# Softmax denominators of a cross-attention: sums of probability tiles on VectorE and GpSimd in place of ones matmuls

## What is computed

```python
# per batch element and head; q: 512 x 8, k and v: 154 x 8 (218 x 8 in layer 0)
s = q @ k.T / sqrt(8)                      # masked keys get -inf
p = exp(s - max(s, axis=keys))             # unnormalised probabilities
o = (p @ v) / sum(p, axis=keys)            # the denominator is what the change touches
x = x + concat_heads(o) @ Wo + bo
```

## Time and profile before

| | |
|---|---|
| median of 3 runs | 964.61 us (962.47 to 964.93) |
| the profiled execution | 964.95 us |
| its span, first to last instruction | 963.2 us |
| attention items of layers 0 and 1 | 46 to 363 us |
| feed-forward of layer 1 | 363 to 540 us |
| attention items of layer 2 | 540 to 656 us |
| feed-forward of layer 2, then layer 3 | 656 to 963 us |
| instructions | 15428 |

### The profile page before, as it was taken

One profiled execution on the slowest core, in us unless ns is written; L12 is line 12 of the kernel. 1 busy time (PEld: TensorE's weight loads), 2 busy tenths in 40 slices (PEclk: granted clock), 3 DMA queues, 4 the chain that ended last, 5 costly groups with the idle time before them and its releaser, 6 DMA issues. The chain is left out here.

```text
span 963.2 us, 15428 instructions
## 1 busy us (share of the span) xinstructions
PE 890.3 (92%) x5522; PEld 635.3 (66%) x5522; DVE 574.8 (60%) x1401; ACT 444.9 (46%) x799; POOL 275.6 (29%) x402
## 2 busy tenths in 40 slices
PE   3799999999999998999989899998999999999994
PEld 3555464655565536889877655545888888888783
DVE  2866758574866756454546477765536344454478
ACT  7265574757574654243322456755224232222350
POOL 6321407263766441011111145432001000021152
PEclk9999999998999999999999899999999999999997
DMA  5000000001020110000000210100000000000001
GB/s 159 7 2 15 1 17 1 15 2 37 2 56 11 71 37 24 1 1 1 1 1 1 81 36 26 53 25 14 2 1 1 1 1 1 2 1 1 1 1 44
DMA packets 27573, 18.10 MB, mean 19 GB/s; under 512 B 6221, under 2 KB 25770, under 8 KB 27370
## 3 DMA queue, kind: packets, MB, share of 16 engines
q1 hardware_dynamic: 27498, 17.12, 6.3%
HBM read 15.63 MB, written 1.05 MB: 17 GB/s over the span
## 5 line engine op out<-in xcount | busy, mean ns | idle before, releaser
L1377 DVE TENSOR_REDUCE mneg<-PS 128x2 f32<-128x308 f32 (+1 forms) x384 | 180.1, 515 | 107.2 <-PE PS L913 106.3
L1848 ACT ACTIVATE work<-PS 128x512 f32<-128x512 f32 (+2 forms) x168 | 100.0, 597 | 249.0 <-PE PS L1104 235.3
L1546 DVE TENSOR_TENSOR work<-PS,work 128x512 f32<-128x512 f32 (+2 forms) x168 | 114.8, 685 | 166.3 <-PE PS L1104 122.6
L1825 ACT ACTIVATE work<-PS 124x512 f32<-124x512 f32 (+1 forms) x272 | 157.1, 601 | 89.3 <-PE PS L1039 88.2
L1118 PEld LDWEIGHTS PS<-down_w,work 128*128 128x128 f32 (+2 forms) x1344 | 157.9, 191 | 5.7 <-DVE work L1546 1.3
L1118 PE MATMUL PS<-down_w,work 128*128 128x128 f32 (+2 forms) x1344 | 158.5, 275 | 1.0 <-DVE work L1546 1.0
L1102 PE MATMUL PS<-xh_sb,arena 128*128 128x512 f32 (+2 forms) x336 | 138.0, 411 | 8.8 <-DVE work L1546 8.7
L1104 PE MATMUL PS<-xh_sb,arena 128*128 128x512 f32 (+2 forms) x336 | 132.7, 395 | 0.0
L1103 PE MATMUL PS<-xl_sb,arena 128*128 128x512 f32 (+2 forms) x336 | 132.1, 393 | 0.0
L1926 POOL TENSOR_SCALAR rstd<-bn_mv 128x4 f32<-128x4 f32 x32 | 7.6, 238 | 423.1 <-DVE bn_mv L1275 423.0
L913 PEld LDWEIGHTS PS<-kb_sb,qxt_sb 97*128 97x128 f32 x256 | 44.0, 190 | 61.6 <-DVE mneg L1377 28.7
(11 more groups left out here) (217 smaller groups left out, 1248.5 us busy)
## 6 DMA issues: line engine op xcount, KB each, us to landing
ctx_rep<-in_ctxT SPq DMA_DIRECT2D x12, 308.0 KB, 3.3
stage<-in_w SPq DMA_DIRECT2D x8, 256.0 KB, 3.9
stage<-in_wg SPq DMA_DIRECT2D x8, 176.0 KB, 2.5
stage<-in_wu SPq DMA_DIRECT2D x8, 176.0 KB, 2.4
x_res<-in_x SPq DMA_DIRECT2D x4, 256.0 KB, 5.4
down_w<-in_w SPq DMA_DIRECT2D x1, 1024.0 KB
down_w<-in_wd SPq DMA_DIRECT2D x8, 128.0 KB
out<-x_res SPq DMA_DIRECT2D x4, 256.0 KB, 2.3
```

Of the source, the lines that this page charges most:

```text
L1377: dve.tensor_reduce(mneg[:, a % 2, t, h0:h0 + 2], PS[:, bank_of["mx", a, m], 0:2 * (KT0 if layer == 0 else KC)].rearrange("p (h n) -> p h ...
L1546: dve.tensor_tensor(HH[0:rows, e % 2, j, :], PS[0:rows, 2 * (n % 2) + 1, :], SS[0:rows, n % 2, :], ALU.mult).then_inc(*sig["h"].mark((i, n)))
L1825: act.activation(p_tile(i, n)[0:rows, :], PS[0:rows, n % 2, :], ACT.Exp, scale=SCALE).then_inc(*sig["p"].mark((i, n)))
L1848: act.activation(SS[0:rows, n % 2, :], PS[0:rows, bank, :], ACT.Silu).then_inc(*sig["act"].mark((i, n)))
```

## The change

The keys are padded from 154 to 160 and laid out in chunks of 32 keys times four heads, so every chunk has 128 rows and row r belongs to head r // 32 in all of them: 5 chunks of context keys, and 2 more of memory keys in layer 0. The six padding keys get a bias that makes their probability zero. As all chunks have the same layout, the denominators can be formed from the sum of the tiles. For each head group, DVE or POOL adds the tiles of all chunks but the last (`p_sum`), slot by slot; PE applies the 0/1 matrix `MV` once to that sum (slot N - 1) and once to the last chunk's tiles (slot N + 3). The sum for slot m is queued one slot later; which engine does it is in `on_vector`: in layer 0 DVE does 11 and POOL 9, in layers 1 and 2 DVE and POOL do 6 each. An `exps` now waits for the value matmul and for the sum that read the tile before. The maxima are 320 or 448 columns wide. `v_blocks` in layer 0 needs 7 matmuls in place of 13. The replicated context comes from the host in its final layout (`ctxR`), there is one small DMA more (`pad`), and some memsets at the start are gone. Some entries of the slot tables move by one to five slots. The diff, cut to its core:

```diff
+KP = 160
+KH = KP // 2
+KPC = 32
+CC = KP // KPC
...
-R0, C0 = 125, 7
-R1, C1 = 124, 5
-KT0 = KC + KM
+RK = HL * KPC
+C0 = CC + KM // KPC
+C1 = CC
...
+        P3SUM = sb("p_sums", [128, 3, S])
...
+        P_SUM = [P3SUM[:, 0, :], P3SUM[:, 1, :], P3SUM[:, 2, :], work[:, 4096:4608]]
...
+        def on_vector(m):
+
+            return m in (4, 5, 7, 11, 13, 15, 19, 20, 21, 22, 23)
+
+        def sum_signal(m):
+
+            return sig["p_sum_dve" if on_vector(m) else "p_sum"]
+
+        def p_sum(eng, i, m):
+
+            g = m % G
+            eng.wait_ge(*sig["p"].at((i, m)))
+            if m < 2 * G:
+                u = after(i, -1)
+                if is_attn(u):
+                    eng.wait_ge(*sig["dn"].at((u, n_slots(u) - G - 1)))
+                    if g == G - 1:
+                        eng.wait_ge(*on_signal(u).at(u))
+                elif u is not None:
+                    eng.wait_ge(*sig["resid"].at(u))
+            else:
+                eng.wait_ge(*sum_signal(m - G).at((i, m - G)))
+            eng.tensor_tensor(P_SUM[g], p_tile(i, m - G) if m < 2 * G else P_SUM[g], p_tile(i, m), ALU.add).then_inc(
+                *sum_signal(m).mark((i, m)))
...
-                if n % 4 == 3 and n >= 7:
+                if n in (N - 1, N + 3):
                     c = (n - 7) // 4
...
+                        if not last:
+                            pe.wait_ge(*sum_signal(4 * c + g).at((i, 4 * c + g)))
+                        pe.matmul(PS[32 * g:32 * g + 32, 7, :], MV[:, :], p_tile(i, 4 * c + g) if last else P_SUM[g],
+                                  start=not last, stop=last).then_inc(*sig["dn"].mark((i, 4 * c + g)))
...
                 if n >= P_RING:
-                    act.wait_ge(*sig["dn"].at((i, n - P_RING)))
+                    act.wait_ge(*sig["pv"].at((i, n - P_RING)))
+                    m = max(n - P_RING, n % G + G)
+                    act.wait_ge(*sum_signal(m).at((i, m)))
...
+                act.wait_ge(*sig["dn"].at((i, n_slots(i) - G - 1)))
                 act.activation(VS, PS[:, 6, :], ACT.Copy).then_inc(*sig["vs"].mark(i))
...
+                    m = n - 1
+                    if kind == "A" and G <= m < n_slots(i) - G and on_vector(m):
+                        p_sum(dve, i, m)
...
+                    m = n - 1
+                    if ITEMS[i][0] == "A" and G <= m < n_slots(i) - G and not on_vector(m):
+                        p_sum(pool, i, m)
```

More of the change, by code:

```diff
@@ L144, in n_slots @@
     if kind == "A":
[L145 removed]
+        return 4 * chunks_of(layer)
     return {"F0": 4, "F1": 16, "F2": 26, "A3": 4, "F3": 2}[kind]
@@ L837, in v_blocks @@
                 layer, b = a // B, a % B
-                rows, chunks = chunk_shape(layer)
                 if part == 0:
@@ L845, in v_blocks @@
                 wait_for(bank)
-                for c in range(4 * part, min(4 * part + 4, chunks)):
-                    o = PS[0:rows, bank, (c % 4) * D:(c % 4 + 1) * D]
-                    cols = slice(c * rows, (c + 1) * rows)
-                    mem = layer == 0 and (c + 1) * rows > KC
-                    mm = pe.matmul(o, CR[:, a % 2, cols], WA[:, layer % 2, 2, :], start=True, stop=not mem)
-                    if mem:
-                        mm = pe.matmul(o, MR[:, cols], ident[:, :], start=False, stop=True)
+                for c in range(4 * part, min(4 * part + 4, chunks_of(layer))):
+                    o = PS[0:RK, bank, (c % 4) * D:(c % 4 + 1) * D]
+                    if c < CC:
+                        mm = pe.matmul(o, CR[:, a % 2, c * RK:(c + 1) * RK], WA[:, layer % 2, 2, :], start=True, stop=True)
+                    else:
+                        mm = pe.matmul(o, MR[:, c - CC, :, :].rearrange("p h n -> p (h n)"), ident[:, :], start=True, stop=True)
                 mm.then_inc(*sig["v_psum"].mark((a, part)))
@@ L1023, in attention_step @@
                 a = layer * B + b
-                rows, chunks = chunk_shape(layer)
+                chunks = chunks_of(layer)
                 N = 4 * chunks
@@ L1038, in attention_step @@
                         pe.wait_ge(*taken[n % 2])
-                    pe.matmul(PS[0:rows, n % 2, :], KB(layer)[0:K_ALL, a % 2, g, c * rows:(c + 1) * rows],
+                    pe.matmul(PS[0:RK, n % 2, :], KB(layer)[0:K_ALL, a % 2, g, c * RK:(c + 1) * RK],
                               QXT[0:K_ALL, a % 2, g, :], start=True, stop=True).then_inc(*sig["st"].mark((i, n)))
@@ L1050, in values @@
                 a = layer * B + b
-                rows, chunks = chunk_shape(layer)
+                chunks = chunks_of(layer)
+                N = 4 * chunks
                 if n % 4 == 1 and n >= 5:
@@ L1063, in values @@
                         taken[6] = sig["vs"].at(i) if is_attn(after(i, 1)) else on_signal(i).at(i)
-                if n % 4 == 3 and n >= 7:
+                if n in (N - 1, N + 3):
                     c = (n - 7) // 4
-                    mask = MV0 if layer == 0 else MV1
-                    if c == 0 and 7 in taken:
+                    last = n == N + 3
+                    if not last and 7 in taken:
                         pe.wait_ge(*taken[7])
                     for g in range(G):
-                        pe.matmul(PS[32 * g:32 * g + 32, 7, :], mask[0:rows, c, :], p_tile(i, 4 * c + g)[0:rows, :],
-                                  start=(c == 0), stop=(c == chunks - 1)).then_inc(*sig["dn"].mark((i, 4 * c + g)))
+                        if not last:
+                            pe.wait_ge(*sum_signal(4 * c + g).at((i, 4 * c + g)))
+                        pe.matmul(PS[32 * g:32 * g + 32, 7, :], MV[:, :], p_tile(i, 4 * c + g) if last else P_SUM[g],
+                                  start=not last, stop=last).then_inc(*sig["dn"].mark((i, 4 * c + g)))
                     if c == chunks - 1:
@@ L1297, in v_mask @@
                 layer = a // B
-                rows, chunks = chunk_shape(layer)
-                mask = MV0 if layer == 0 else MV1
-                c0, c1 = 4 * part, min(4 * part + 4, chunks)
+                c0, c1 = 4 * part, min(4 * part + 4, chunks_of(layer))
                 dve.wait_ge(*sig["v_psum"].at((a, part)))
@@ L1815, in exps @@
                 _, layer, b = ITEMS[i]
-                rows, _ = chunk_shape(layer)
                 act.wait_ge(*sig["st"].at((i, n)))
@@ L2127, in constants @@
     c["maskk"] = m
-    heads0 = sum([[h] * KT0 for h in range(HL)], [])
-    ctx0 = ([1] * KC + [0] * KM) * HL
-    heads1 = sum([[h] * KC for h in range(HL)], [])
-    for name, heads, isctx, rows, chunks in (("0", heads0, ctx0, R0, C0), ("1", heads1, [1] * len(heads1), R1, C1)):
-        mv = np.zeros((rows, chunks, G, HL, HD), np.float32)
-        for r, (h, ic) in enumerate(zip(heads, isctx)):
-            mv[r % rows, r // rows, :, h, :] = 1
-        c["mv" + name] = mv.reshape(rows, chunks, G, HL * HD)[:, :, 0, :]
+    mv = np.zeros((HL, KPC, HL, HD), np.float32)
+    for h in range(HL):
+        mv[h, :, h, :] = 1
+    c["mv"] = mv.reshape(RK, HL * HD)
+    pad = np.zeros((2, KH), np.float32)
+    pad[1, KC - KH:] = PAD
+    c["pad"] = pad.T
     inv = np.float32(10000.0) ** (np.arange(0, HD, 2, dtype=np.float32) / np.float32(HD))
```

185 lines of the change are left out of this document (89 added, 96 removed), and 32 rows, old and new, of tables (SLOTS, SLOTS0).

## The result

The changed kernel takes 1032.4 us (1032.0 to 1035.6, four runs) against 964.7 for the kernel before: a ratio of 1.071, 95% interval [1.069, 1.074]. It is 68 us slower, where the prediction said 20 us faster. Its profiled execution took 1035.6 us with a span of 1033.7.

The account below looks back on a forecast made before the run. PE was taken as the bound, but not by much. 964.95 us, less 32.7 in the items, plus 8 (POOL's queue), 4 (clock) and 1 (start), gave 945.2, stated as 945.0; forecast 936 to 951 (0.41), wider range 923 to 972.

Parts of the forecast that it names:

- PE's relief: PE in the attention items: 44 fewer ones-matmul groups save 48.0 us, the shorter `v_blocks` 3.9, together 51.9 us.
- The rule of the larger of two: Attention items: each lasts the larger of PE's rest and DVE's work / 0.95; 400.3 us for 433, 32.7 less.
- the case that I had named as what would make the forecast wrong: Attention items: DVE's share under 0.85 while items don't shrink; then waits between engines, not work, set the time.
- The port: DVE's sums with two SBUF inputs wait for POOL's reads: 0.25 us per sum, between 0 and 0.76.
- The clock: PE's granted clock: a PE that waits more gets more 1.2 GHz stretches; 4 us lost, between 0 and 10.
- POOL's queue: POOL in attention items: lateness of work queued with its sums costs 8 us, between 0 and 17.
- At nothing: Other moved slots, `kb_out` in two instructions, `values_out` with one more wait, and strided key columns: priced at nothing.
- The start: Kernel start: one more small DMA ahead of the first matmul's weights, and 32 wider maxima, cost 1 us.
- The third, on the other side: Each DVE sum pays a whole POOL operation, 1.46 us; 990.4 us, decides from 1.17 us per sum; chance 0.18.
- The first rival: PE's saving arrives nearly whole: sums seldom meet POOL's work, POOL keeps up, the clock stays; 918.7 us; chance 0.15.

Follow-up runs that it names:

- no_sums: Changed kernel without any sums: ones matmuls only for each item's last two chunks, the other chunks' part of the denominators left out; 951.0 us, ratio 0.986.
- pool_writes: Changed kernel with each of POOL's 84 sums replaced by three memsets that read nothing; DVE's sums stay; 994.2 us, ratio 1.032.
- dve_part: Changed kernel with DVE's sums kept and POOL's replaced, after the first item, by an 8-column memset behind the same waits; 982.3 us, ratio 1.019.
- pool_part: Changed kernel with POOL's sums as three memsets and DVE's replaced by 8-column memsets behind the same waits, first item's sums real; 985.2 us, ratio 1.022.
- vector_psum_all: Changed kernel with all 176 sums on DVE, none on POOL, each reading one operand from PSUM; 1006.3 us, ratio 1.044.
- waits_only: Changed kernel with every sum on DVE and POOL replaced by an 8-column memset behind the same waits; 955.4 us, ratio 0.991.
- psum_operand: Changed kernel with DVE's 92 sums reading one operand from PSUM, POOL's sums kept; 1003.9 us, ratio 1.041.
- sums_kept_ones: Changed kernel with all sums and waits, but PE makes every chunk's ones matmuls again and the sums are not read; 1036.3 us, ratio 1.076.
- all_pool: Changed kernel with all 176 sums on POOL, none on DVE; 1103.0 us, ratio 1.144.

## Why the prediction was wrong

**PE's relief: the term was 12 us too large, and its use wrong.** I put 51.9 us; PE's work at full clock fell by 40 (`no_sums`). I let it shorten the items one for one where DVE allowed it. With nothing added it shortened the kernel by 13.7 us, and beside the sums by some 4.

**The rule of the larger of two was the step that failed.** I let an item last as long as PE's rest or DVE's work / 0.95, whichever is more. Even with the measured 1.10 us per sum in place of 0.95 the same working gives 412 us for the items, and 957 for the kernel, not 1032. DVE is at 0.75 to 0.80 in the items that lose most. The row maxima hold four PSUM banks that all of PE's side work goes round in, DVE serves them in order, and POOL's chains feed both. What the runs show in the rule's place is PE idle behind row maxima, long before DVE is full: 13.7 us before, 20.8 in `no_sums`, 35.5 in `pool_writes`, 62.5 after. Work added on DVE or POOL isn't absorbed up to 0.95. `dve_part` and `pool_part` put a price on it: 67 us of sums on DVE cost 14 to 19 us (some of it still the port), and 102 us of memsets on POOL cost 17 to 24, which is 0.17 to 0.29 of their length, with neither engine a bound anywhere; 120 us on DVE cost 0.43 of itself (`vector_psum_all`). That the ring of banks is how the delay reaches PE is read from the code and the traces; no run has more banks. In the items that lose most, that is the case that I had named as what would make the forecast wrong: DVE under 0.85 and items that don't shrink.

The whole account, by medians: 964.7, less 13.7 for the work taken off PE (`no_sums`), plus 4.4 for the waits (`waits_only`), plus 38.9 for the work on DVE and POOL with what is left of the port (`pool_writes`), plus 38.2 for the port against POOL's sums, is 1032.4.

**The port: mechanism right, upper bound wrong.** I took 0.25 us per sum between 0 and 0.76. The mean was 1102 - 762 = 0.34, or 0.42 over the 680 ns of `psum_operand`, inside. But 0.76, the whole of one POOL operation, is no upper bound: holds reach 5.66 us on a sum and 7.37 on other work. In rows 8 the POOL subtraction is the last of its run, and POOL idles 3.25 us behind it; where POOL's queue is full, no such gap comes for DVE to slip into. I also priced only the sums, while L1404 and others are held too: DVE's busy time has 45.5 us of it in all. What `pool_writes` takes away of it cost 38.2 us.

The Trainium skill, page SBUF — State Buffer, section "Who interferes with whom", says that the one that comes second waits until the first instruction finishes. The traces agree that it waits, but in them a hold spans seven POOL instructions in a row.

**The clock: 4 us predicted, 37 measured**, by the balance. I priced a stretch at half of 3.4 us and all new ones together at 10 at most. In the first 700 us the stretches at 0.50 sum to 34.1 us before and to 112.6 after. The sign was right, the size came from counting stretches that exist instead of asking how many long waits the change would make. The Trainium skill, page TensorE: Matmul & The Clock Gate, Part 1, has throttled as the default and activity as what releases it; here `sums_kept_ones` agrees, with 48 us less at 1.2 GHz when PE has more to do.

**POOL's queue: 8 us predicted, 0 to 17.** Measured: 17 to 24 (`pool_part`). Its shares in the third to sixth items were 0.65 to 0.69, below the 0.76 to 0.89 that I had worked out for shorter ones, so they were no guide to its lateness.

**At nothing:** the layout's edits are, as predicted. The moved slots are not: +10.8, -2.8 or -13.7 us by what runs beside them. The start came 0.5 us earlier, where I had 1 us more.

**The rivals.** The third, on the other side, had the right cause and sign with 990.4. By its own mark, a mean over 1.17 us, it would have been denied at 1.10: the mean of the sums hid the few long holds and left out those of DVE's other work. That its 990.4 comes nearer than my forecast is in part luck, since 42 us are still missing. Where it fell short is the other half, the queues: a sum by item has no term for them, and from 994.2 down the port had 7.5 us of excess left in the 92 sums; what that costs from end to end was not measured. The first rival, at 918.7, lay 32 us below what even `no_sums` reaches.

## What to carry to other kernels

Before moving work off the bounding engine, run the kernel with the work simply left out: here that was worth 13.7 us, not 52, so with these slot tables no way of doing it elsewhere could have won more. In an in-order ring of few buffers, price work that is added to any engine at a share of its length well below saturation (here 0.17 to 0.29 for the first 67 to 102 us, and 0.43 for 120 us on DVE), and look at the longest instance of a held instruction and what waits behind it, not at the mean. Add to PE's new idle time what the clock takes besides, here half as much again.

## What the runs showed of the hardware

- A DVE operation on SBUF can be held across many back-to-back POOL operations: 7.37 us over seven of them in the changed kernel, 10.19 us over ten in `all_pool`. Both ended within the last POOL instruction of a gapless run, which lasted 1.70 us in place of 1.25. POOL's memsets, which only write, did not do it: beside them the 92 sums had a mean of 762 ns and a longest of 1602, with POOL's other work still reading. With one operand in PSUM (`psum_operand`) none of them took over 693.
- A DVE operation with one tensor input of 80x32 was held as well (4.20 and 7.85 us, for 0.18 us free).
- POOL pays too: its 84 sums had a mean of 1432 ns in the changed kernel and 1285 in `psum_operand`, where DVE's sums read PSUM; 27 of them took over 1.6 us, for 2.
- A kernel in which PE does 44 us more work took some 4 us more, as PE idled 19 us less and the granted clock rose from 0.932 to 0.958.
